# Attention row sums on one Trainium2 core: three partial sums a head become two, with a ring of ten probability tiles

## The reference

```
mod = silu(c) @ wmod                         # six rows: sa, ca, ga, sb, cb, gb
h = layernorm(x) * (1 + ca) + sa
q, k, v = split(h @ Wqkv.T)                  # 16 heads of 32, for 2 sequences
ctx = softmax(q k.T / sqrt(32)) v            # 2048 x 2048 scores for each of 32 heads
x = x + ga * (ctx @ Wproj.T + bproj)
h = layernorm(x) * (1 + cb) + sb
x = x + gb * (hadamard(silu(h @ W1.T) * (h @ W3.T)) @ W2.T)
```

## Time and profile before

| what | value |
|---|---|
| time, median of 3 runs | 3243.02 us (3241.72 to 3248.1) |
| time of the profiled run | 3243.02 us |
| its span | 3241.2 us |
| TensorE busy | 3146.9 us, 97% |
| VectorE busy | 1848.7 us, 57% |
| ScalarE busy | 1515.0 us, 47% |
| GpSimd busy | 1284.4 us, 40% |
| accumulating carries | 186 of 1 MB |

### The profile page before, as it was taken

One profiled execution on the slowest core, in us unless ns is written; L12 is line 12 of the kernel. 1 busy time (PEld: TensorE's weight loads), 2 busy tenths in 40 slices (PEclk: granted clock), 3 DMA queues, 4 the chain that ended last, 5 costly groups with the idle time before them and its releaser, 6 DMA issues. The chain is left out here.

```text
span 3241.2 us, 42015 instructions
## 1 busy us (share of the span) xinstructions
PE 3146.9 (97%) x15868; PEld 2124.6 (66%) x15868; DVE 1848.7 (57%) x3153; ACT 1515.0 (47%) x2852; POOL 1284.4 (40%) x480
## 2 busy tenths in 40 slices
PE   6999799999999999999999997979999999999998
PEld 5877455555555555555555552758888888888887
DVE  4444487788788787887887861643323323233232
ACT  3333156666666666666766664443222222222221
POOL 2222067777787777777777870000000000000000
PEclk8999689999999999999999998989999999999999
DMA  6665548888888888888888873652212112121111
GB/s 232 194 192 170 145 102 165 176 184 174 172 184 175 179 178 175 183 174 175 182 174 175 185 151 84 238 206 88 81 56 71 44 59 72 33 72 46 59 59 33
DMA packets 148633, 445.37 MB, mean 137 GB/s; under 512 B 26833, under 2 KB 44497, under 8 KB 113362
## 3 DMA queue, kind: packets, MB, share of 16 engines
q0 software_dynamic: 28448, 203.44, 31.0%
q1 hardware_dynamic: 118930, 239.25, 25.1%
q10 hardware_dynamic: 1056, 0.00, 0.0%
HBM read 166.85 MB, written 80.21 MB: 76 GB/s over the span
## 5 line engine op out<-in xcount | busy, mean ns | idle before, releaser
L1071 DVE TENSOR_REDUCE mxp<-pmax 128x1 f32<-128x512 f32 x2048 | 1251.1, 680 | 298.2 <-PE pmax L892 298.2
L1033 ACT ACTIVATE prob<-pexp 128x512 f32<-128x512 f32 x2048 | 1031.4, 624 | 449.0 <-PE pexp L937 446.7
L892 PE MATMUL pmax<-kst,qst 96*128 96x512 f32 x2048 | 856.9, 426 | 19.0 <-DMA v<-v_scratch 16.5
L937 PE MATMUL pexp<-qst,kst 98*128 98x512 f32 x2048 | 818.6, 402 | 3.1 <-ACT prob L1033 3.1
L892 PEld LDWEIGHTS pmax<-kst,qst 96*128 96x128 f32 x2048 | 396.8, 194 | 319.6 <-DVE mxp L1071 166.0
L1144 POOL TENSOR_TENSOR gsum<-gsum,prob 128x2048 f32<-128x2048 f32 x124 | 577.2, 4655 | 22.4 <-ACT prob L1033 13.5
L1144 POOL TENSOR_TENSOR gsum<-prob 128x2048 f32<-128x2048 f32 x93 | 429.8, 4622 | 198.9 <-ACT prob L1033 198.7
L946 PE MATMUL pctx<-prob,v 128*32 128x512 f32 x4096 | 494.6, 599 | 0.0
L937 PEld LDWEIGHTS pexp<-qst,kst 98*128 98x128 f32 x2048 | 386.4, 189 | 139.8 <-ACT prob L1033 21.4
L1653 DVE TENSOR_TENSOR hid<-sil,pl 128x512 f32<-128x512 f32 x128 | 88.0, 688 | 638.6 <-PE pl L51 631.0
L51 PE MATMUL pg<-h2f,w 128*128 128x512 f32 x1536 | 371.1, 391 | 1.0 <-issue 1.0
(11 more groups left out here) (118 smaller groups left out, 1688.8 us busy)
## 6 DMA issues: line engine op xcount, KB each, us to landing
gsum<-prob POOLq DMA_DIRECT2D x186, 1024.0 KB, 7.8
w<-w_scratch SPq DMA_DIRECT2D x128, 256.0 KB, 2.6
qst<-q_scratch SPq DMA_DIRECT2D x96, 256.0 KB, 4.2
kst<-k_scratch SPq DMA_DIRECT2D x96, 256.0 KB, 6.2
xin<-in_L_attn_query_dram SPq DMA_DIRECT2D x16, 1024.0 KB, 8.6
q_scratch<-obq SPq DMA_DIRECT2D x32, 512.0 KB, 5.0
k_scratch<-obq SPq DMA_DIRECT2D x32, 512.0 KB, 3.7
v_scratch<-vst SPq DMA_DIRECT2D x8, 1024.0 KB, 5.6
```

The costliest lines, as they stand in the source:

```text
L892: pe.matmul(pmax[:, bank, :], qst[0:KR, slot, qt * P:(qt + 1) * P], kst[0:KR, slot, kc * TOK:(kc + 1) * TOK], start=True, stop=True).then_ ...
L937: pe.matmul(pexp[:, score_bank(g, n), :], kst[:, slot_of(g), kt * P:(kt + 1) * P], qst[:, slot_of(g), j * TOK:(j + 1) * TOK], start=True, ...
L1033: act.activation(prob_tile(g, kt)[:, j * TOK:(j + 1) * TOK], pexp[:, score_bank(g, n), :], ACT.Exp, scale=SCALE).then_inc(exp_done, 1)
L1071: dve.tensor_reduce(mxp[:, par, u // QJ, u % QJ:u % QJ + 1], pmax[:, bank, :], X, ALU.max).then_inc(mx_done, 1)
```

## The change

It sorts the 16 key tiles of a head anew. Before, GpSimd adds 4, 2 and 4 tiles into three partial sums (7 additions), and six carries go to sums 0, 1, 0, 1, 0, 1. After, GpSimd adds 5 and 5 tiles into two partial sums (8 additions), and six carries go to sums 0, 0, 1, 0, 1, 0. Each sum has two buffers. The `prob` ring grows from 9 to 10 tiles, `gsum` shrinks from 5 tiles to 4. The units of a head move from behind score 31 of the next head to behind score 39. The load of head g + 2 waits no longer for 16 exponentials of head g. GpSimd's order is rewritten.

```diff
-SLOTS, RING = 3, 9
-BUFS = (2, 2, 1)
+SLOTS, RING = 3, 10
...
-POOLED = ((0, 1, 2, 3), (5, 6), (7, 9, 11, 13))
-CARRIED = (4, 8, 10, 12, 15, 14)
-CARRY_TO = (0, 1, 0, 1, 0, 1)
+POOLED = ((0, 1, 2, 3, 4), (5, 6, 8, 9, 11))
+CARRIED = (7, 10, 12, 13, 14, 15)
...
-TURN_AFTER, UNIT_AFTER = 48, 31
+TURN_AFTER, UNIT_AFTER = 48, 39
 INVERT_AT = 36
-LOAD_AT = 16
...
-    LAST_CARRY = [max([i for i, k in enumerate(CARRY_TO) if k == n], default=None) for n in range(UNITS)]
+    CARRY_TO = (0, 0, 1, 0, 1, 0)
+    LAST_CARRY = [max(i for i, k in enumerate(CARRY_TO) if k == n) for n in range(UNITS)]
...
-        gsum = sb("gsum", [P, sum(BUFS), S])
+        gsum = sb("gsum", [P, UNITS, 2, S])
...
-            return gsum[:, sum(BUFS[:k]) + g % BUFS[k], :]
+            return gsum[:, k, g % 2, :]
...
                         sp.wait_ge(pv_done, KT * g)
-                        sp.wait_ge(exp_done, NM * g + LOAD_AT)
                         load(g + 2, slot_of(g + 2))
...
-                    if LAST_CARRY[k] is None:
-                        pe.wait_ge(add_done, ADDS * g + adds_until(POOLED[k][-1]))
-                    else:
-                        pe.wait_ge(merged[LAST_CARRY[k]], 16 * (g + 1))
+                    pe.wait_ge(merged[LAST_CARRY[k]], 16 * (g + 1))
...
-                        if g >= BUFS[k]:
-                            pool.wait_ge(unit_done, UNITS * (g - BUFS[k]) + k + 1)
+                        if g >= 2:
+                            pool.wait_ge(unit_done, UNITS * (g - 2) + k + 1)
...
-                    for m in (1, 2, 3):
+                    for m in (1, 2, 3, 4):
                         add(g, 0, m)
                     carry(g, 0)
                     add(g, 1, 1)
+                    add(g, 1, 2)
                     carry(g, 1)
-                    add(g, 2, 1)
+                    add(g, 1, 3)
+                    add(g, 1, 4)
                     carry(g, 2)
-                    add(g, 2, 2)
                     carry(g, 3)
                     if g >= 2:
                         divide(g - 2)
-                    add(g, 2, 3)
                     carry(g, 4)
                     carry(g, 5)
```

## The result

The changed kernel takes 3425.22 us (median of 4; 3422.76 to 3426.93), the kernel before 3244.49 us (median of 4; 3241.72 to 3248.1). The ratio is 1.0556, 95% interval 1.0537 to 1.0574: 181 us, 5.6%, slower. The forecast was 3400, range 3315 to 3505. The profiled run took 3422.41 us, its span is 3420.6.

The account below looks back on a forecast made before the run. TensorE bounds the kernel before; after the change GpSimd's chain would, at 54.6 us a head. 31 x (54.6 - 49.5) = 157 us on 3243.02 gives 3400 us, the saved 26.9 not subtracted; range 3315 to 3505.

Parts of the forecast that it names:

- What bounds the kernel: Attention stage before the change: TensorE busy throughout at full clock, each unit 0.87 us, one fewer saving 26.9 us over 31 heads.
- GpSimd's chain becomes the bound: GpSimd's new order: its shortest period, 41.7 us plus tile 13's landing time, exceeds the 48.37 us TensorE wants per head.
- Where it comes out: ScalarE's exponential of tile 9 waits for the slot of the previous head's tile 15, 5 to 6 us each head.
- The formula 31 (C - 49.5): Time difference over 31 heads, C being GpSimd's period per head: 157 us slower at C = 54.6.
- the formula's constant: Start of head 31 after the change, put at 409.2 + 31 C, against 1944.4 before.
- The sum for C: GpSimd's period: 40.85 us to tile 13's carry, plus x, plus 0.87 for tile 15's carry; 54.6 us.
- x: Tile 13's time from carry issue to landing: 12.0 us, middle of the pairs, plus 0.9 for loads, 12.9.
- The landing of tile 15: Its carry, issued when tile 13 lands, queues behind that of 14 and lands two transfers, 10.0 us, later.
- a figure for x (16): Tile 13's landing by the skill's round-robin rule alone: near 16 us, period 57.7, time an estimated 3497.
- Costed at nothing: Tenth ring tile, smaller gsum, earlier tiles' slots, second sum buffers and later units: no added cost.
- The clock: TensorE's clock falls in each head's 6 us pause, hidden; rival: staying at 1.2 GHz gives 4700 us, chance 0.02.
- What the profile was to show: L1155 transfer waits about 300 us, first additions 54 to 55 apart, unit records 744 to 496, transfer share about 0.77.

Follow-up runs that it names:

- experiment 8: Kernel before without its third unit's matmuls on TensorE, that partial sum missing from the row sums: 3214.63 us, ratio 0.9904.
- experiment 2: Changed kernel with the carries of tiles 12 and 13 parted by the last addition, 12 and 14 to sum 0, 13 and 15 to sum 1: 3334.63 us.
- 1: Changed kernel with the carry of tile 15 issued behind the next head's first addition: 3315.0 us, ratio 1.0221.
- 5: Changed kernel without the addition of tile 11, which is missing from the row sums: 3284.85 us, ratio 1.0121.
- 10: Changed kernel with carry 14 behind the next head's first addition, 15 behind its second, and loads held until 24 exponentials: 3230.1 us, ratio 0.9961.
- experiment 3: Changed kernel with the loads held back until 24 exponentials of the head are done: 3419.73 us, ratio 1.0535.
- 4: Changed kernel with loads held until 24 exponentials and the division moved behind the carry of tile 15: 3419.29 us (one run).
- 9: Changed kernel with the carry of tile 14 behind the next head's first addition and 15 behind its second, loads still early: 3311.64 us, ratio 1.0205.
- 10 to 12: Changed kernel with both last carries moved into the next head, loads held until 24, 28 and 32 exponentials: 3230.1, 3237.35 and 3240.98 us.
- 7: Kernel before with its units behind score 39 in place of 31: 3246.41 us, ratio 1.0000.
- 6: Kernel before with the second wait of its loads taken out, so they are issued early: 3244.09 us, ratio 0.9999.

## Why the prediction was right, point by point

- *What bounds the kernel:* TensorE, with 0.87 us for each unit. Shown by experiment 8: without one unit, 26 to 36 us less where 26.9 was worked out.
- *GpSimd's chain becomes the bound.* Shown. Parting the pair (experiment 2) and taking the wait for tile 13 nearly out (1) took away 91 and 111 us with all additions in place; one addition fewer (5) took away its own 4.7 us a head. With eight additions, hardly a wait for a landing on GpSimd and the loads held (10) the period is 48.8.
- *Where it comes out.* Shown: 143.9 us of waits in ScalarE, 30 times, 29 of them ahead of tile 9, the tile that was named; 4.8 us each, where 5 to 6 was said.
- *The formula 31 (C - 49.5).* It gives 186 us for the changed kernel (181 measured), 179 for experiment 3 (174), 182 for 4 (173), 93 for 2 (89), 41 for 5 (39), 62 for 1 (70) and 58 for 9 (66). It holds within 9 us. In experiment 9 GpSimd follows TensorE again, so there the formula is no explanation. Nor does it fit 10 to 12, which have hardly any lag: 22, 21 and 19 us under the kernel before by the formula, 16, 9 and 6 measured. The 5 us between 186 and 181 are the formula's constant: head 31's exponentials begin at 2124.5 us, where 409.2 + 31 x 55.5 is 2129.7.
- *The sum for C was 0.9 us short, and one term had the wrong reason.* In the mean of heads 3 to 28 tile 13 is issued 41.1 us into a head (40.85 in the sum), lands 13.2 us later (x, 12.9), the carry of 15 is issued 0.6 us after that landing (a step that the sum does not have), and the next head begins 0.57 us behind it (0.87): 55.5 in place of 54.6. That is 28 us by the formula, and 25 us lie between 3400 and 3425. In x, 0.9 us was put down for the loads. Experiments 3 and 4 show that in the lagging state it was the context stores, 1.2 us, and hardly the loads, 6 us in the whole kernel. That the wrong reason gave nearly the right size is luck; without the term the forecast would have been 28 us lower, still in the range. I had not looked at what the division sets off: it stands directly behind the pair in the new order, and its stores follow at once.
- *The landing of tile 15 was put at 10.0 us and took 16.6.* That is the mean of heads 3 to 28, with the loads beside it; in heads 29 and 30, which have no loads beside them, it took 10.6 and 11.1. So the loads cost this carry 6 us. The time does not show it, because in this order GpSimd never waits for tile 15, and the landing enters the reckoning of the time only once, at the end.
- *The Trainium skill's* "DMA: Bandwidth & Descriptors" (Queues, rings and completion order) says that an engine goes round robin between queues with work. The trace agrees in kind: with the stores beside it tile 13 lands after 13.1 us, without them after 12.0 (3 and 4), and loads beside carries take longer as well, a median of 12.5 us to landing for the parts of q in the changed kernel where it was 4.2. As a figure for x (16) it was too high, since loads and pair hardly met: in SyncE's order the loads come behind the stores. In the head of the timeline the stores go out at 1191.26 and the first loads at 1197.05, and until tile 13 lands at 1201.7 that queue has moved 0.26 MB, no more than the stores.
- *Costed at nothing.* The later units and the early loads are shown to cost nothing in the kernel before (7, 6). But early loads are not free in every order: with both carries late, 24 exponentials of waiting were worth 81 us (9 against 10). The ring and the buffers were not tried by themselves.
- *The clock.* As forecast, it fell and was hidden. Windows of one head, columns as in the earlier trace rows:

```profile
1102.00:1108.00 6.00, 1.77 (x8) 1.12 (x6) 3.51 (x7) 0.92 (x2) 5.86 (x2) 0.80 0.94 228
1108.00:1114.00 6.00, 5.13 (x33) 1.44 (x33) 0.00 (x0) 2.67 (x5) 5.45 (x3) 0.64 0.40 97
1114.00:1126.00 12.00, 12.00 (x73) 6.60 (x65) 10.20 (x19) 8.05 (x16) 11.86 (x4) 1.00 0.60 120
```

  After 5 us of pause the granted clock is partly 0.50 (1.2 GHz; 0.64 in the mean of the second window), and full again in the third. "TensorE: Matmul & The Clock Gate" of the Trainium skill (HAM oscillation) warns of just that, and by its rule the trace agrees. That it costs nothing in the changed kernel follows from C, which is set by GpSimd; it was not tried by itself. Where GpSimd waits for exponentials it was not free (9).
- *What the profile was to show.* Right: the units' records (744 before, 496 after), the transfer share (0.71 to 0.79 in four windows; 0.77 was said), the first additions 55 us apart. Off in the booking: I expected about 300 us of L1149's waits under the transfers, and only 56.5 stand there; the rest is booked on exponentials, because GpSimd waits for both. Its idle time before the last two carries, 4.7 and 5.8 us a head in the mean of heads 3 to 28, makes the 10 us a head that were said.

## What to carry to other kernels

When an engine executes a hand-written order that issues transfers and waits for their landing, write down its period as a sum, work and waits together, and compare it with the period of the bound; a busy share of 78% says nothing about it. Work that is saved on the bound engine is worth it only up to that sum. Move dependent issues to where their condition has long been met, behind the next unit's first work, and then look again at which transfers meet.

## What the runs showed that I had not expected

- In the changed kernel an addition of 128 x 2048 float32 that starts at once behind an issued carry takes 4.9 us and not 4.6 (mean 4.888 us for the 62 that start a sum; 4.616 for the others, of which 31 also stand behind a carry). It is no cost: from the issue to the end of the addition it is 5.46 us (1167.24 to 1172.70), and in the earlier trace rows it was 5.47 (1027.88 to 1033.35), where the addition itself took 4.65 but began later.
- The pause shows in the units: they come directly after it in each head, at the lower clock, and a record of L956 takes 0.989 us in the mean, where L962 of before took 0.596.
- Four stores of 64 KB, a quarter of a carry's megabyte, took 1.2 us of the transfer engines' time beside a carry, a quarter of what a whole carry ahead of it costs (5 us).
- Of the groups below (changed kernel, 400 to 2300 us) the first two are the same line and show the first of these; the third shows how the carries' waits are booked:

```profile
L1138 POOL TENSOR_TENSOR gsum<-gsum,prob 128x2048 f32<-128x2048 f32 x186 | 858.6, 4616 | 22.6 <-ACT prob L1027 0.5
L1138 POOL TENSOR_TENSOR gsum<-prob 128x2048 f32<-128x2048 f32 x62 | 303.1, 4888 | 61.3 <-ACT prob L1027 61.3
L1149 POOL DMA_DIRECT2D gsum<-prob x186 | 161.4, 913 | 362.8 <-ACT prob L1027 280.3 <-DMA gsum<-prob 56.5 <-POOL gsum L1138 19.7
```
